# Moving ranks, beta and statistics around the opening products of a conditional residual MLP kernel

## The reference

```python
h = relu(x @ W1[lang] + b1[lang])
a = x + h @ W2[lang] + b2[lang]
x = x + layernorm(a) * gamma[lang] + beta[lang]          # called x1 below
s_m = relu(x @ share_wi[m]) @ share_wo[m]                # m = 0, 1, 2, D = 128, F = 512
out_a, out_b = the same with expert type and type + 1, weighted by softmax(10 * gate_vecs)
g = softmax(relu(concat(first tokens of expert_out, s_0, s_1, s_2) @ gate_w1) @ gate_w2)
out = x + expert_out * g_0 + s_0 * g_1 + s_1 * g_2 + s_2 * g_3
```

## Time and profile before

| | |
|---|---|
| median of 3 runs | 85.42 us (84.96 to 85.45) |
| profiled execution | 83.69 us, of which the span is 81.9 us |
| TensorE (PE) busy | 76.0 us, 93% of the span |
| VectorE (DVE), ScalarE (ACT), GpSimd (POOL) busy | 56.8, 55.9, 41.1 us |
| chain that ended last | PE 78%, POOL 8%, DVE 4%, ACT 3% |
| granted TensorE clock | full (0.99 mean) |

### The profile page before, as it was taken

How to read it: one execution, slowest core, us unless ns; L and a number is a source line. 1 busy time by engine, 2 the same in 40 slices (tenths; PEclk the granted TensorE clock), 3 DMA queues, 4 the chain that set the end, 5 groups by cost and what they waited for, 6 DMA issues and landing times.

```text
span 81.9 us, 1646 instructions
## 1 busy us (share of the span) xinstructions
PE 76.0 (93%) x458; PEld 64.1 (78%) x458; DVE 56.8 (69%) x163; ACT 55.9 (68%) x138; POOL 41.1 (50%) x86
## 2 busy tenths in 40 slices
PE   4998969999999999999999999999999999999950
PEld 1366547678868999888999988888999898999720
DVE  4368977999669465375345664579758997589960
ACT  0728996996996999996899964644726565286310
POOL 4883041699798986278975400000005893039700
PEclk9999999999999999999999999999999999999995
DMA  0794866999978893000000000000000000220004
GB/s 3 168 183 60 259 177 141 353 306 343 324 236 226 204 313 107 0 0 0 8 0 0 0 0 0 0 4 0 0 0 8 0 0 0 64 64 8 0 4 128
DMA packets 12150, 7.56 MB, mean 92 GB/s; under 512 B 2500, under 2 KB 10968, under 8 KB 12140
## 3 DMA queue, kind: packets, MB, share of 16 engines
q1 hardware_dynamic: 11984, 7.39, 31.9%
q0 software_dynamic: 96, 0.05, 0.4%
q10 hardware_dynamic: 60, 0.01, 0.1%
HBM read 5.87 MB, written 0.52 MB: 78 GB/s over the span
## 4 chain that ended last, share of the span: by engine, by line
PE 78%; POOL 8%; DVE 4%; ACT 3%; issue 2%; ACTq 0%; POOLq 0%
PE bank L1057 11%; PE bank L1060 11%; PE bank L1058 11%; PE bank L1012 10%; PE bank L1013 10%; PE bank L1014 10%; PE bank L1091 4%; POOL prod L517 3%; PE bank L1085 2%; PE bank L1065 2%; POOL prod L519 2%; PE bank L940 2%; POOL wl L473 2%; PE bank L950 1%; PE bank L975 1%
## 5 line engine op out<-in xcount | busy, mean ns | idle before, releaser
L823 DVE SCALAR_TENSOR_TENSOR hl<-bank,hh 128x256 fp32r<-128x256 f32 (+2 forms) x60 | 31.4, 526 | 15.7 <-ACT hh L602 15.2
L602 ACT ACTIVATE hh<-bank 128x256 fp32r<-128x256 f32 (+2 forms) x60 | 28.1, 470 | 12.6 <-PE bank L1014 11.9
L473 POOL TENSOR_TENSOR wl<-w_raw,wh 128x512 fp32r<-128x512 f32 x18 | 23.1, 1294 | 11.4 <-ACT wh L595 11.4
L1060 PE MATMUL bank<-hl,wh 128*128 128x256 f32 (+2 forms) x60 | 20.2, 336 | 0.1
L1057 PE MATMUL bank<-hh,wh 128*128 128x256 f32 (+2 forms) x60 | 19.8, 330 | 0.1
L1058 PE MATMUL bank<-hh,wl 128*128 128x256 f32 (+2 forms) x60 | 19.6, 326 | 0.0
L1060 PEld LDWEIGHTS bank<-hl,wh 128*128 128x128 f32 x60 | 11.3, 189 | 1.6 <-DVE hl L823 0.7
L1057 PEld LDWEIGHTS bank<-hh,wh 128*128 128x128 f32 x60 | 11.4, 189 | 1.2 <-issue 0.5
L1058 PEld LDWEIGHTS bank<-hh,wl 128*128 128x128 f32 x60 | 11.4, 189 | 0.7
L595 ACT ACTIVATE wh<-w_raw 128x512 fp32r<-128x512 f32 x18 | 11.3, 629 | 0.0
L1012 PE MATMUL bank<-x1hl,wh 128*128 128x256 f32 (+1 forms) x34 | 11.2, 329 | 0.0
(11 more groups left out here) (118 smaller groups left out, 108.4 us busy)
## 6 DMA issues: line engine op xcount, KB each, us to landing
w_raw<-in_L_cond_expert_wi_dram SPq DMA_DIRECT2D x6, 256.0 KB, 4.1
w_raw<-in_L_cond_expert_wo_dram SPq DMA_DIRECT2D x6, 256.0 KB, 4.5
w_raw<-in_L_cond_share_wi_dram SPq DMA_DIRECT2D x3, 256.0 KB, 3.0
w_raw<-in_L_cond_share_wo_dram SPq DMA_DIRECT2D x3, 256.0 KB, 3.3
x_in<-in_x_dram SPq DMA_DIRECT2D x2, 256.0 KB, 3.4
xs<-x1hl SPq DMA_DIRECT2D x4, 128.0 KB, 3.8
x1hl<-xs SPq DMA_DIRECT2D x4, 128.0 KB, 2.8
out_dram<-o_sb SPq DMA_DIRECT2D x4, 128.0 KB, 1.8
```

Source lines behind the costliest of these rows:

```text
L473: nc.gpsimd.tensor_tensor(wl[:, k, w, :], w_raw[:, k, buf(w), :], wh[:, k, w, :].bitcast(f32), ALU.subtract).then_inc(s_wl[w], 1)
L602: nc.scalar.activation(packed(hh[:, u % NBUF, :], r), packed(h_ps[u % NBUF][:, :], r), ACT.Relu).then_inc(s_hh, 1)
L823: nc.vector.scalar_tensor_tensor(out=packed(hl[:, u % NBUF, :], r), in0=packed(h_ps[u % NBUF][:, :], r), scalar=0.0, in1=packed(hh[:, u % ...
L1060: nc.tensor.matmul(dst, wh[:, 1, w, chunk], lo, start=False, stop=(c == FC - 1)).then_inc(s_mm2, 1)
```

## The change

It moves work between places in the opening, in five parts.

- VectorE: `sort_by_type` is cut in three. `slot_tables` stays where it was. `compare_types` (`key`, `sq`) stands ahead of x1T of pair 0, and `sort_by_type` (the ranks' sum and cast) behind it. Ranks get a semaphore of their own, `s_rank`; whoever loads ranks waits for it. ScalarE loads them all in unit 2.
- The first matrix of set 0 is cast, and its residual taken, in two halves of 256 columns (`first_high`, `first_low`). The opening products wait for the first half; the first product of unit 2 waits for both.
- ScalarE: beta of sequences 4 and 5 moves from ahead of the deviations to behind the cast of set 0's second matrix, next to that of 6 and 7. Both first deviations go ahead of the adapter's ReLU for the second half.
- VectorE: the statistics of pair 3 move behind `hidden_low(0)`, and `types` behind `hidden_low(4)`. ScalarE's deviation of pair 3 moves behind a cast of unit 0.
- TensorE: `residual(3)` moves behind `transpose_z(1)`.

```diff
+        def part_of(i):
+            return slice(i * F // 2, (i + 1) * F // 2)
...
             for k in range(RING):
                 load_slot(k)
+            sp.wait_ge(s_rank, 1)
             ranks = loaded(sp, "rank", tab_i[0:1, 0:B], [B - 1] * B)
...
+            def first_low(i):
+
+                pool.wait_ge((s_w0h, s_wh[0])[i], 1)
+                nc.gpsimd.tensor_tensor(wl[:, 0, 0, part_of(i)], w_raw[:, 0, 0, part_of(i)],
+                                        wh[:, 0, 0, part_of(i)].bitcast(f32),
+                                        ALU.subtract).then_inc((s_w0l, s_wl[0])[i], 1)
...
             pick_adapters()
-            pool.wait_ge(s_tab, 1)
+            first_low(0)
+            first_low(1)
+            pool.wait_ge(s_rank, 1)
             ranks = dict(zip(range(HB, B), loaded(pool, "rank", tab_i[0:1, HB:B], [B - 1] * HB)))
-            weights_low(0, (0,))
             pool.wait_ge(s_x1l, PAIRS // 2)
             weights_low(0, (1,))
...
             nc.scalar.activation(xT[:, cols(1)], xt_ps[1][:, :], ACT.Copy).then_inc(s_xtc[1], 1)
-            add_beta((4, 5))
             standard_deviation(0)
+            standard_deviation(1)
             adapter_relu(1)
-            standard_deviation(1)
-            weights_high(0, 0)
+            first_high(0)
             normalised()
             x1_high(0)
+            first_high(1)
             x1_high(1)
             weights_high(0, 1)
+            add_beta((4, 5))
             add_beta((6, 7))
-            act.wait_ge(s_tab, 1)
-            ranks = dict(zip(range(HB, B), loaded(act, "rank", tab_i[0:1, HB:B], [B - 1] * HB)))
             for u, (r, c) in enumerate(UNITS):
                 hidden_high(u)
                 if u == 0:
                     standard_deviation(2)
-                    standard_deviation(3)
                 if u < 2:
                     weights_high(1, u)
+                if u == 0:
+                    standard_deviation(3)
...
-            sort_by_type()
+            slot_tables()
             norm_stats(0)
             norm_stats(1)
             norm_apply(0)
             norm_apply(1)
             dve.wait_ge(s_colsc, 1)
+            compare_types()
             x1_transposed(0)
+            sort_by_type()
             x1_transposed(1)
             x1_low(0)
             x1_low(1)
-            types()
             norm_stats(2)
-            norm_stats(3)
             for u, (r, c) in enumerate(UNITS):
                 hidden_low(u)
 
+                if u == 0:
+                    norm_stats(3)
+                if u == 4:
+                    types()
...
             transpose_z(0)
-            residual(3)
             adapter_out(2)
             transpose_z(1)
+            residual(3)
             adapter_out(3)
             opening_products()
```

More of the change, by code:

```diff
@@ L270, in conditional_residual_mlps @@
         s_tab = sem("s_tab")
+        s_rank = sem("s_rank")
+        s_w0h = sem("s_w0h")
+        s_w0l = sem("s_w0l")
         s_wseq = sem("s_wseq")
@@ L591, in x1_high, with first_high @@
                                      x1T[:, pair(n)].rearrange("p (b s) -> p b s", s=S), ACT.Copy).then_inc(s_x1h, 1)
+            def first_high(i):
+                act.wait_ge(s_wi[0], 16)
+                nc.scalar.activation(wh[:, 0, 0, part_of(i)], w_raw[:, 0, 0, part_of(i)],
+                                     ACT.Copy).then_inc((s_w0h, s_wh[0])[i], 1)
             def weights_high(w, k):
@@ L669, in _ @@
                 if u == 2:
-                    ranks.update(zip(range(HB), loaded(act, "rank_", tab_i[0:1, 0:HB], [B - 1] * HB)))
+                    act.wait_ge(s_rank, 1)
+                    ranks = dict(enumerate(loaded(act, "rank", tab_i[0:1, 0:B], [B - 1] * B)))
+                    act.wait_ge(s_tab, 1)
                     starts = loaded(act, "start", tab_i[0:1, place(0, 0):place(SLOTS, 0)],
@@ L734, in down, with slot_tables @@
                 return v.unsqueeze(2).to_broadcast([P, v.shape[1], n])
-            def sort_by_type():
+            def slot_tables():
                 dve.wait_ge(s_kind, 16)
                 dve.wait_ge(s_seqno, 1)
-                no_b = seq_no[:, 0:B]
                 link(nc.vector.tensor_copy(kind_f[:, :], kind_p[:, :]))
@@ L744, in sort_by_type @@
                 tt(reached[:, :, :], down(split[:, :], NK), across(seq_no[:, :], 2), ALU.is_ge)
-                stt(key[:, :], kind_f[:, :], float(B), no_b, ALU.mult, ALU.add)
-                tt(sq[:, :, :], across(key[:, :], B), down(key[:, :], B), ALU.is_lt)
-                total(tab[:, 0:B], sq[:, :, :])
                 dve.wait_ge(s_steps, sum(len(at) for at in STEPS.values()) + 2)
@@ L752, in sort_by_type, with compare_types @@
                       taken[:, :, :, :].rearrange("p s (w i) k -> p s w i k", w=2))
-                nc.vector.tensor_copy(tab_i[:, :], tab[:, :]).then_inc(s_tab, 1)
+                nc.vector.tensor_copy(tab_i[:, B:], tab[:, B:]).then_inc(s_tab, 1)
+            def compare_types():
+                stt(key[:, :], kind_f[:, :], float(B), seq_no[:, 0:B], ALU.mult, ALU.add)
+                tt(sq[:, :, :], across(key[:, :], B), down(key[:, :], B), ALU.is_lt)
+            def sort_by_type():
+                total(tab[:, 0:B], sq[:, :, :])
+                nc.vector.tensor_copy(tab_i[:, 0:B], tab[:, 0:B]).then_inc(s_rank, 1)
             def types():
@@ L773, in load_ranks @@
             def load_ranks(lo, hi):
-                dve.wait_ge(s_tab, 1)
+                dve.wait_ge(s_rank, 1)
                 return dict(zip(range(lo, hi), loaded(dve, f"rank{lo}_", tab_i[0:1, lo:hi], [B - 1] * (hi - lo))))
@@ L996, in first_product @@
                     pe.wait_ge(s_wl[w], 1)
+                if u == FC // 2:
+                    pe.wait_ge(s_wh[w], 1)
+                    pe.wait_ge(s_wl[w], 1)
                 if run == ("slot", 0) and c == 0:
@@ L1018, in opening_products @@
                 w = set_of(0)
-                pe.wait_ge(s_wh[w], 1)
-                pe.wait_ge(s_wl[w], 1)
+                pe.wait_ge(s_w0h, 1)
+                pe.wait_ge(s_w0l, 1)
                 for n in range(PAIRS // 2):
```

## The result

The kernel after takes 85.34 us, the kernel before 84.94 beside it (medians of 23 runs each, 84.98 to 87.28 and 83.83 to 85.76). The ratio is 1.0078 with a 95% interval of [1.0049, 1.0107]: slower by 0.66 us. In six of the fourteen profiles TensorE takes some 1.7 times as long for its matmuls until about 10 us (1.12 us for four transposes instead of 0.66), at a granted clock of 1.00 (2.4 GHz) all the same; ratios and, from here on, medians leave out the executions that are longer by over 1.5% than the fastest of their kernel, as these are, but the one profiled for the kernel after is among them (86.6 us), so its opening stands some 1.75 us late on every compute engine. Counted so, the kernel after has a median of 85.05 us and the kernel before of 84.50: 0.55 apart, where the ratio gives 0.66.

The account below looks back on a forecast made before the run. The end was set by when TensorE's dense stream starts, its length and its few waits. Terms +1.16 - 0.31 - 0.05 gave +0.80 us on a median of 85.42: 86.2 us, range 85.4 to 87.0.

Parts of the forecast that it names:

- Chain to unit 1: Opening: `hh` of unit 1 waits for the fourth pair's statistics and deviation, so `hl` of unit 1 ends 1.16 us later.
- the lock: VectorE with two SBUF inputs and GpSimd reading SBUF share a port exclusively; the later one blocks until the first ends.
- Absorbed at `xs`: TensorE's stall before its first product on the sorted copy, laid to SyncE's copies, fills with 0.31 us of the delay.
- Statistics earlier: VectorE's second-pair statistics start 0.05 us earlier once the ranks' 0.71 us are moved; TensorE's y holds the rest.
- Lock at the comparison: Rival, chance 0.2: GpSimd's first half starts before VectorE's rank comparison and delays the chain 0.40 us, sum +1.20 us.
- Lock at x1's low part: VectorE's low part of x1 for pair 0 meets GpSimd's second half and takes about 0.8 us; hidden before unit 0.
- Nothing absorbed: Rival, chance 0.12: the stall at 24.1 is not the copies' or they move too, so the sum is +1.11 us.
- Not slower, through the ranks' cut: Rival, chance 0.14: the 0.71 us cut on VectorE brings the whole opening forward, leaving +0.14 us, 85.6.
- Faster by over 1%: Rival, chance 0.06: opening comes forward, the fourth pair's deviation is off the path, and copies land 0.9 us earlier.
- Halves: First weights cast on ScalarE and subtracted on GpSimd in two halves: nothing saved, nothing lost.
- Types at unit 4: 0.18 us of VectorE moved to where `hl` has about 0.8 us of cover: 0 to 0.2 us, taken as 0.
- `residual(3)` behind the second transposes: TensorE's moved transposes, 0.22 us, start the opening products at 13.0 for 12.8; the next waits until 13.58 anyway: nothing.

Follow-up runs that it names:

- e3: The kernel after with both beta of sequences 4 and 5 and the fourth pair's statistics back at their old places: 1.0015 of the kernel before, 84.19 us.
- e6: The kernel before with the cut of the ranks alone: 0.9964 of the kernel before, 84.67 us.
- e5: The kernel after with the four xs copies issued ahead of the slot load in front of them: 1.0041 of the kernel before, 85.20 us.
- experiments 1 to 3: Three runs of the kernel after with parts undone, as ratios to the kernel before: statistics back 1.0019, beta back 1.0060, both back 1.0015.
- e2: The kernel after with beta of sequences 4 and 5 back at its old place, statistics still moved: 1.0060 of the kernel before, 84.73 us.
- e4: The kernel before with the four xs copies issued ahead of the fourth slot's weight loads: 0.9968 of the kernel before, 83.87 us.
- e9: The kernel before with the xs copies issued early, run again in the third batch as a base: 0.9932 of the kernel before, 83.91 us.
- e12: The kernel after with beta and statistics at their old places and the xs copies early: 0.9944 of the kernel before, 84.00 us.
- e10: The kernel before with early xs copies and the first set's weights in halves: 0.9985 of the kernel before, 84.00 us.

## Why the prediction was right

Direction, mechanism and place were right. The change was put at +0.80 us and measured at +0.66 by the ratio, +0.55 by the medians. The time itself was not met as well: 86.2 us lies 0.86 above the plain median of the kernel after, 85.34, which is just below the 85.4 where the range began. Of the 0.86, 0.48 is the base (the three runs shown had a median of 85.42, the 23 beside the kernel after 84.94) and the rest is the change, 0.40 between the plain medians where 0.80 was forecast. Set upon the 85.42 that the prediction started from, the ratio gives 86.09. The chances favoured a loss of over 1%, at 0.50; the 0.78% measured lies within 1%, which had 0.44.

That the size came near was partly luck: it took the stall of one execution, 0.31 us, for the stall of all, and counted in the same way e3 had 0.64 and e6 1.23.

The steps show best in e5, whose opening is the kernel after's and is not late by 1.75 us:

```profile
11.65 0.61 DVE L838 SCALAR_TENSOR_TENSOR x1T<-bank,cols_c,xT_beta 128x128 f32<-128x128 f32 x2
...
12.71 0.61 DVE L838 SCALAR_TENSOR_TENSOR x1T<-bank,cols_c,xT_beta 128x128 f32<-128x128 f32 x2
13.24 1.21 DVE L846 TENSOR_TENSOR x1hl<-x1T,x1hl 128x256 fp32r<-128x256 f32 x2
...
15.98 0.69 DVE L852 SCALAR_TENSOR_TENSOR hl<-bank,hh 128x512 fp32r<-128x512 f32 x1 [0.91 <-ACT hh L623]
...
18.19 0.69 DVE L852 SCALAR_TENSOR_TENSOR hl<-bank,hh 128x512 fp32r<-128x512 f32 x1
```

```profile
14.20 1.26 ACT L588 ACTIVATE xT_beta<-xT,cols_c 128x128 f32<-128x128 f32 x4
15.37 0.57 ACT L623 ACTIVATE hh<-bank 128x512 fp32r<-128x512 f32 x1
...
17.38 0.29 ACT L575 ACTIVATE deviation<-mv,eps 128x2 f32<-128x2 f32 x1 [0.73 <-DVE mv L813]
17.58 0.58 ACT L623 ACTIVATE hh<-bank 128x512 fp32r<-128x512 f32 x1
```

All of it is 0.16 us late from the first x1T on (11.65 for 11.49), since TensorE's y products waited 0.35 us for a load of weights. Less this:

- Chain to unit 1, +1.16: `hh` 0 at 15.21 (forecast 15.23), `hl` 0 at 15.82 (15.86), deviation at 17.22 (17.20), waiting 0.73 us (0.8), `hh` 1 at 17.42 (17.39), `hl` 1 at 18.03 (18.00). The last stands 1.19 us later than before. The third matmul of unit 1's second product starts at 18.94 as measured (18.8), the first `xs` product at 25.21 (near 25) without a stall. By experiments 1 to 3 some 0.77 us of it are the statistics, 0.29 the beta and 0.14 the rest. At `hh` of unit 0 the beta and the lock together make 0.56, of which the lock alone would make 0.23 (e2: 14.88 for 14.65). The prediction gave the beta 0.58 and called the lock hidden; both hold, but undoing the beta brings back only the part of it that the lock doesn't take in its place.
- Absorbed at `xs`, -0.31: the mis-sized term. The prediction took the copies' landing for a fixed point near 24.1. It is none: the first product that waits for them stood at 24.08 in the profile of before, at 24.55 in e3, 25.04 in e2 and 25.13 in e6, with no change to the copies. Nor is it the 0.31 us of the one profile: 1.19 - 0.66 = 0.5 us by the measured difference, 0.3 to 0.6 by what early copies gave the kernel before (e4, e9). The prediction had 85.4 us for a floor on its account, which it is not: an earlier issue on SyncE moved it.
- The lowest runs show the chain without the stall: 84.98 after and 83.83 before, 1.15 us apart; with early copies 84.81 and 83.74, 1.07 apart.
- Statistics earlier, -0.05: it came, as 0.63 us behind TensorE's products for 0.68, but only 0.02 of it reached the second x1T (e6). The prediction had 0.04 for the key and the comparison right behind it and left that out of the sum. The sum and cast fit between the two x1T, and the statistics were bounded by TensorE's y, as argued.
- Lock at the comparison (rival, 0.2): it did not happen. The comparison at 12.96 in the kernel after is followed by x1T at 13.22 as any small instruction would be; VectorE was first, by 0.09 us (GpSimd's half starts at 13.05) where 0.07 was forecast.
- Lock at x1's low part: forecast 0.8, measured 0.87 us. GpSimd's half costs 0.73, not half of 1.29.
- Nothing absorbed (rival, 0.12): wrong on the mean, right for the fastest executions.
- Not slower, through the ranks' cut (rival, 0.14): refuted by e6's profile. Faster by over 1% (rival, 0.06) needed the same advance.
- Halves: forecast at nothing, which left out what the lock costs once the beta no longer hides it.
- Types at unit 4 and `residual(3)` behind the second transposes: no cost shows. e12 has both and enters `xs` at 24.07, as e10 does, which has neither.

## What to carry to other kernels

Before moving work behind an instruction, follow the moved work's own result: here statistics were put behind `hl` of unit 0, and `hh` of unit 1 waits for them through ScalarE's queue. A stall behind a DMA hides losses elsewhere and varies from run to run, so size small changes against a base without it. Undoing one part of a change shows what that part costs with the others in place: a second cost may have been waiting behind it.

## What the hardware showed that I had not expected

- Four copies of 128 KB, issued at the same times (from 17.3 us) behind the same loads, took 3.8 us at the median to land in one execution (before) and 4.7 in another (e6), the slowest of the four 4.4 and 5.4. Issued about 1 us earlier they took 3.3 to 3.7 at the median in seven profiles, the slowest 4.6 (e4).
- A GpSimd subtraction of 256 columns takes 0.73 us, one of 512 columns 1.29: some 0.17 us don't shrink with the size (2 x 0.73 - 1.29).
- In the kernel after, the VectorE subtraction that took 0.87 us began 0.15 us behind a GpSimd one and ended 0.29 us behind its end, sooner than after the 0.41 us that it takes alone. Begun 0.09 us ahead of GpSimd's other half, VectorE's comparison (0.22 us) and that half (0.73 us) both took as long as elsewhere.
